# Bias rows added by TensorE, a shorter normalisation and a re-staged quantised FFN in a joined decoder kernel

## The reference

```python
def _layernorm(x, axis=-1, eps=1e-05):
    m = jnp.mean(x, axis=axis, keepdims=True)
    v = jnp.var(x, axis=axis, keepdims=True)
    return (x - m) / jnp.sqrt(v + eps)
...
    h = xmid + h                     # 128 features wide
    h = h @ w_up.T + b_up            # back to 1024
    return x_init + jnp.transpose(h, (1, 0, 2))
...
def _dynamic_quant(x, inv_smooth):
    xs = x.astype(jnp.float32) * inv_smooth
    scale = jnp.maximum(jnp.max(jnp.abs(xs), axis=-1, keepdims=True) / QMAX, 1e-08)
    q = jnp.clip(jnp.round(xs / scale), -QMAX, QMAX)
    return (q, scale)
...
    qg, sg = _dynamic_quant(x_flat, inv_gate)      # x_flat is bf16
    qu, su = _dynamic_quant(x_flat, inv_up)
    gate_out = _quant_gemm(qg, sg, w_gate, s_wgate)
    up_out = _quant_gemm(qu, su, w_up, s_wup)
    inter = jax.nn.silu(gate_out) * up_out
    inter = jnp.clip(inter, -SWIGLU_LIMIT, SWIGLU_LIMIT).astype(jnp.bfloat16)
    qi, si = _dynamic_quant(inter, inv_inter)
    out = _quant_gemm(qi, si, w_down, s_wdown)
```

## Time and profile before

| | before |
|---|---|
| median of 3 runs | 3969.88 us (3968.72 to 3972.8) |
| profiled execution, its own time | 3982.61 us |
| its span | 3980.8 us |
| PE busy | 3182.8 us (80%), mean granted clock 0.9 |
| DVE busy | 2233.0 us (56%) |
| ACT busy | 1579.2 us (40%) |
| POOL busy | 502.0 us (13%) |

### The profile page before, as it was taken

The page is one execution under the profiler, slowest core; times in us unless marked ns, Lnnn a source line. Parts: engine busy times, 40 slices in busy tenths (PEclk is TensorE's granted clock), DMA queues, the critical chain, the costliest instruction groups (busy, mean ns, idle before and its releaser), DMA issues. The chain is left out here.

```text
span 3980.8 us, 109362 instructions
## 1 busy us (share of the span) xinstructions
PE 3182.8 (80%) x43218; PEld 2136.2 (54%) x43218; DVE 2233.0 (56%) x5375; ACT 1579.2 (40%) x3982; POOL 502.0 (13%) x1854
## 2 busy tenths in 40 slices
PE   7556568644479999999688899999999999985797
PEld 4424135322256666666344666666666666662343
DVE  2656767578855555555421555555555555547455
ACT  2221134444522222222111566666666666652333
POOL 0000321133310000000000000000000000005232
PEclk9576679866789999999899999999999999996799
DMA  2000020110010000000101233333333333320100
GB/s 97 3 1 1 11 45 8 39 52 0 0 45 1 0 0 0 0 0 0 35 29 37 78 91 87 91 90 88 91 87 92 86 92 88 90 84 0 66 32 37
DMA packets 278942, 176.69 MB, mean 44 GB/s; under 512 B 14496, under 2 KB 268016, under 8 KB 278816
## 3 DMA queue, kind: packets, MB, share of 16 engines
q1 hardware_dynamic: 276128, 172.70, 14.8%
q0 software_dynamic: 2752, 3.18, 0.5%
HBM read 165.12 MB, written 13.90 MB: 45 GB/s over the span
## 5 line engine op out<-in xcount | busy, mean ns | idle before, releaser
L1828 PE MATMUL ps<-de_hg,st_at 128*32 128x128 f32 x16384 | 516.3, 275 | 0.3 <-DVE st_at L1990 0.3
L1828 PEld LDWEIGHTS ps<-de_hg,st_at 128*32 128x32 f32 x16384 | 424.5, 110 | 31.6 <-DVE st_at L1990 0.5
L1893 ACT ACTIVATE st_th<-ps,st_sw 128x128 f32<-128x128 f32 x1024 | 292.7, 368 | 248.0 <-PE ps L1800 248.0
L1973 DVE TENSOR_TENSOR st_th<-ps,st_sw 128x512 f32<-128x512 f32 x256 | 177.1, 692 | 155.5 <-PE ps L1800 155.5
L1766 POOL COPY de_ah<-st_at 128x8 f32 (+1 forms) x256 | 50.7, 198 | 1510.2 <-DVE st_at L1990 1510.2
L1247 PEld LDWEIGHTS ps<-sa_xt,w_wq 128*128 128x128 f32 x2048 | 234.7, 194 | 11.0 <-issue 9.2
L1247 PE MATMUL ps<-sa_xt,w_wq 128*128 128x128 f32 x2048 | 237.9, 278 | 1.9 <-ACT sa_xt L1363 1.9
L1318 PE MATMUL ps<-sa_wo,sa_ct 128*128 128x512 f32 x512 | 225.0, 598 | 13.1 <-issue 13.1
L1789 PE MATMUL ps<-st_hk,st_cwt 112*32 112x128 f32 x4096 | 164.7, 278 | 87.9 <-DMA st_hk<-padded_alignments 85.9
L2252 PE MATMUL ps<-rf_wb,rf_sp 128*128 128x512 bf16 x768 | 184.4, 394 | 20.1 <-DVEq L2383 20.1
L1800 PE MATMUL ps<-st_fs,st_waf 32*128 32x128 f32 x4096 | 186.5, 296 | 12.5
(11 more groups left out here) (415 smaller groups left out, 6341.3 us busy)
## 6 DMA issues: line engine op xcount, KB each, us to landing
st_hk<-padded_alignments SPq DMA_DIRECT2D x254, 448.0 KB, 3.6
X<-in_x_dram SPq DMA_DIRECT2D x16, 512.0 KB, 9.0
out_dram<-X SPq DMA_DIRECT2D x16, 512.0 KB, 2.7
w_wq<-in_Wq_perm_dram SPq DMA_DIRECT2D x1, 4096.0 KB
sa_wo<-in_Wo_perm_dram SPq DMA_DIRECT2D x1, 4096.0 KB, 14.2
gate_inputs<-dp_ro SPq DMA_DIRECT2D x16, 256.0 KB, 2.3
st_rin<-gate_inputs SPq DMA_DIRECT2D x128, 32.0 KB, 3.3
rf_wf<-in_weightT_dram SPq DMA_DIRECT2D x8, 512.0 KB, 8.0
```

The source lines that it names most:

```text
L1828: ins = pe.matmul(R[g][32 * q:32 * q + 32, :], at[g][:, b, :], hg[:, BG * g + b, q * P:(q + 1) * P], start=False, stop=(b == BG - 1), tile ...
L1893: ins = act.activation(th[g][:, b, :], sums(g, 0)[:, b // 2, (b % 2) * P:(b % 2 + 1) * P], ACT.Tanh, bias=sw[g][:, b:b + 1])
L1973: dve.tensor_tensor(th[g][:, 4:8, :].rearrange("p (k s) n -> p k s n", s=2), sums(g, 1).rearrange("p k (s n) -> p k s n", s=2), sw[g][:, 4 ...
```

## The change

It has three parts.

The normalisation. DVE makes only the statistics; the semaphore that released POOL after the fifth small operation now follows L99's successor directly. POOL makes four operations a tile in place of thirteen: minus the mean, variance plus epsilon, that to the power −0.5 (the operation `pow`), and the product of the two. All six normalising stages use it.

The bias rows. In `dn` and in `dp` POOL, which has nothing else to do there, makes three bf16 rows out of each fp32 bias row, whose sum is the bias: SP loads it into partitions 0, 32 and 64 of a cleared tile, and POOL casts, copies one row and subtracts, twice, over 128x1024. In `up` and `yy` each half tile gets a second matmul, of bf16 ones (128x128) with these rows (128x512), into the same PSUM bank. The addition of the bias on DVE and its broadcast load go.

The quantised FFN. The smoothing goes from POOL to DVE, next to the search for the scale, and `v` has one buffer for each of gate and up. TensorE turns the fp32 value that still carries the rounding constant; ACT takes the constant off as it copies the turned tile out of PSUM to bf16. The clips, the casts of L1000 and L1035 and DVE's copy L1066 go. The gate's sixteen turns become 8 + 4 before the gate and 4 between gate and up. DVE forms the row of tile b in the loop of tile b. SP loads the smoothing rows first.

```diff
-        link(dve.bn_aggr(self.agg[:, k, :], self.stats[:, k, :, :]))
-        v, y, nm = self.vy[:, k, 0:1], self.vy[:, k, 1:2], self.vy[:, k, 3:4]
-        link(dve.tensor_scalar(v, self.agg[:, k, 1:2], LN_EPS, None, ALU.add))
...
-        dve.tensor_scalar(nm, self.agg[:, k, 0:1], -1.0, None, ALU.mult).then_inc(self.var_done, 1)
+        dve.bn_aggr(self.agg[:, k, :], self.stats[:, k, :, :]).then_inc(self.agg_done, 1)
...
-        for step in range(3):
-            link(pool.tensor_tensor(q, y, y, ALU.mult))
-            link(pool.tensor_tensor(q, q, v, ALU.mult))
-            link(pool.tensor_tensor(q, q, self.c15[:, :], ALU.add))
-            link(pool.tensor_tensor(self.rs[:, k, 0:1] if step == 2 else y, y, q, ALU.mult))
+        pool.tensor_tensor(nm, self.agg[:, k, 0:1], minus, ALU.mult)
+        link(pool.tensor_tensor(v, self.agg[:, k, 1:2], eps, ALU.add))
+        link(pool.tensor_tensor(self.rs[:, k, 0:1], v, power, ALU.pow))
         pool.tensor_tensor(self.rs[:, k, 1:2], nm, self.rs[:, k, 0:1], ALU.mult).then_inc(self.rstd_done, 1)
...
+class BiasRows:
...
+        sp.wait_ge(self.cleared, 1)
+        for p in (0, 32, 64):
+            sp.dma_start(self.raw[p:p + 1, :], src.rearrange("(o n) -> o n", o=1)).then_inc(self.loaded, 16)
...
+        for p in (0, 32):
+            link(pool.tensor_copy(self.part[:, :], self.raw[:, :]))
+            link(pool.tensor_copy(self.rows[p:p + 1, :], self.part[p:p + 1, :]))
+            link(pool.tensor_tensor(self.raw[:, :], self.raw[:, :], self.part[:, :], ALU.subtract))
+        pool.tensor_copy(self.rows[64:65, :], self.raw[64:65, :]).then_inc(self.ready, 1)
...
+    def add(self, pe, out, h):
+        return pe.matmul(out, self.ones[:, :], self.rows[:, h * 512:(h + 1) * 512], start=False, stop=True)
...
-                            ins = pe.matmul(ps[:, 2 * (b % 2) + h, :], hm[:, b, :], w_up[:, h * 512:(h + 1) * 512],
-                                            start=True, stop=True)
+                            pe.matmul(ps[:, 2 * (b % 2) + h, :], hm[:, b, :], w_up[:, h * 512:(h + 1) * 512],
+                                      start=True, stop=False)
+                            ins = up_bias.add(pe, ps[:, 2 * (b % 2) + h, :], h)
...
-                            link(dve.tensor_tensor(r, r, b_up[:, :].unsqueeze(1), ALU.add))
...
+                for k in range(4):
+                    ins = pe.transpose(ps[:, (0, 1, 2, 0)[n], k * P:(k + 1) * P],
+                                       v[:, j, (4 * h + k) * P:(4 * h + k + 1) * P], ident[:, :])
+                ins.then_inc(t_done, 1)
...
+            def off(act, dst, src):
+                return act.activation(dst, src, ACT.Identity, bias=rnd[:, 1:2])
...
                     act.wait_ge(rci_done, b + 1)
                     act.activation(vi[:, :], vi[:, :], ACT.Identity, bias=rnd[:, 0:1], scale=rc[:, 2 + k:3 + k]).then_inc(added_i, 1)
...
+                    off(act, qit[:, :, :].rearrange("p k n -> p (k n)"), ps[:, TI, :]).then_inc(qit_done, 1)
+                    if has(b + 1):
+                        add_round(act, b + 1, 0)
+                        add_round(act, b + 1, 1)
+                        keep_gate(act, b + 1)
+                        keep_up(act, b + 1)
...
+                link(dve.tensor_tensor(v[:, j, :], xh[:, k, :], inv[:, j, :], ALU.mult))
+                if j == 1:
+                    dve.sem_inc(read, 1)
+                find_scale(dve, link, v[:, j, :], j, rc_done)
...
-                            link(dve.tensor_tensor(r, ps[:, 4 + 2 * k:6 + 2 * k, :].rearrange("p a n -> p (a n)"), lyb[:, :], ALU.add))
+                            link(dve.tensor_tensor(r.unsqueeze(1), ps[:, 4 + 2 * k:6 + 2 * k, :].rearrange("p a n -> p (a n)").unsqueeze(1),
+                                                   X[:, bass.ds(b, 1), :], ALU.add))
                             dve.sem_inc(o_used, 1)
-                            link(dve.tensor_tensor(r.unsqueeze(1), r.unsqueeze(1), X[:, bass.ds(b, 1), :], ALU.add))
```

More of the change, by code:

```diff
@@ L122, in apply, with __init__, work_in, load @@
                        bias=self.rs[:, k, 1:2], scale=self.rs[:, k, 0:1]).then_inc(self.row_free, 1)
+class BiasRows:
+    def __init__(self, kept):
+        self.rows = kept.sb("b3", [P, HID], BF16)
+        self.ones = kept.sb("ones16", [P, P], BF16)
+    def work_in(self, work):
+        self.raw, self.part = work.sb("b_raw", [P, HID]), work.sb("b_part", [P, HID], BF16)
+        self.cleared, self.loaded, self.seq, self.ready = work.sems("b_cleared b_loaded b_seq b_ready")
+    def load(self, sp, src):
+        sp.wait_ge(self.cleared, 1)
+        for p in (0, 32, 64):
+            sp.dma_start(self.raw[p:p + 1, :], src.rearrange("(o n) -> o n", o=1)).then_inc(self.loaded, 16)
+    def split(self, pool):
+        link = Chain(pool, self.seq)
+        pool.memset(self.raw[:, :], 0.0).then_inc(self.cleared, 1)
+        pool.memset(self.ones[:, :], 1.0).then_inc(self.ready, 1)
+        link(pool.memset(self.rows[:, :], 0.0))
+        pool.wait_ge(self.loaded, 48)
+        for p in (0, 32):
[3 more added lines that the diff above has]
+        pool.tensor_copy(self.rows[64:65, :], self.raw[64:65, :]).then_inc(self.ready, 1)
+        pool.wait_ge(self.ready, 2)
+    def add(self, pe, out, h):
+        return pe.matmul(out, self.ones[:, :], self.rows[:, h * 512:(h + 1) * 512], start=False, stop=True)
 SEQ = NB
@@ L928, in _ @@
             def _(pool):
-                pool.wait_ge(w_load, 96)
-                def smooth(b, k):
-                    pool.wait_ge(staged, b + 1)
-                    if not (isinstance(b, int) and b < 2):
-                        pool.wait_ge(q_done, 2 * b - 2)
-                    for j in range(2):
-                        pool.tensor_tensor(v[:, k, j, :], xh[:, k, :], inv[:, j, :], ALU.mult).then_inc(scaled, 1)
                 ln.start_pool(pool, Chain(pool, pool_seq))
-                for b in range(4):
-                    smooth(b, b % 2)
@@ L941, in _ @@
-                with pool.Fori(0, NB // 2 - 2) as i:
-                    link = Chain(pool, pool_seq, 1 + i * 2 * ln.POOL_LINKS)
+                with pool.Fori(0, NB // 2) as i:
+                    link = Chain(pool, pool_seq, ln.POOL_SETUP + i * 2 * ln.POOL_LINKS)
                     for k in range(2):
                         ln.factors(pool, link, 2 * i + k, k)
-                        smooth(2 * i + 4 + k, k)
-                link = Chain(pool, pool_seq, 1 + (NB - 4) * ln.POOL_LINKS)
-                for b in range(NB - 4, NB):
-                    ln.factors(pool, link, b, b % 2)
@@ L965, in _, with project @@
+            def project(pe, b, j):
+                pe.wait_ge(t_kept, 3 * b + (1, 3)[j])
+                if j == 0:
+                    pe.wait_ge(gu_used, b)
+                for k in range(KH):
+                    ins = pe.matmul(ps[:, GU + j, :], qt[:, j, k, :], (wu if j else wg)[:, k, :],
+                                    start=(k == 0), stop=(k == KH - 1))
+                ins.then_inc(gu_done, 1)
             @block.tensor
@@ new lines, in _, with body @@
+                dve.wait_ge(w_load, 64)
+                FIRST = 6
+                PER = 4 + 2 + 6 + 2 + ln.LINKS
+                state = {"link": link}
+                def body(b, k):
+                    link = state["link"]
+                    dve.wait_ge(gu_done, 2 * b + 1)
+                    dve.scalar_tensor_tensor(out=gu[:, 0, :], in0=ps[:, GU, :], scalar=sc[:, 0:1], in1=swg[:, :],
+                                             op0=ALU.mult, op1=ALU.mult).then_inc(gate_done, 1)
+                    dve.wait_ge(gu_done, 2 * b + 2)
+                    link(dve.scalar_tensor_tensor(out=gu[:, 1, :], in0=ps[:, GU + 1, :], scalar=sc[:, 1:2], in1=swu[:, :],
+                                                  op0=ALU.mult, op1=ALU.mult))
+                    dve.sem_inc(gu_used, 1)
+                    dve.wait_ge(silu_done, b + 1)
+                    link(dve.tensor_tensor(gu[:, 1, :], gu[:, 0, :], gu[:, 1, :], ALU.mult))
+                    link(dve.tensor_scalar(it[:, :], gu[:, 1, :], LIMIT, -LIMIT, ALU.min, ALU.max))
+                    dve.wait_ge(ti_done, b)
+                    link(dve.tensor_tensor(vi[:, :], it[:, :], invi[:, :], ALU.mult))
+                    find_scale(dve, link, vi[:, :], 2 + k, rci_done)
+                    if has(b + 1):
+                        for j in range(2):
+                            smooth(dve, link, b + 1, 1 - k, j)
```

249 lines of the change are left out of this document (103 added, 146 removed).

## The result

The changed kernel takes 3787.78 us (median of 4 runs, 3786.36 to 3788.87) beside 3969.3 us for the kernel before (4 runs): ratio 0.9542, 95% interval 0.9526 to 0.9559, 181.5 us less. The forecast was 3798 us, 171.5 less in its sum, with a range of 3778 to 3840.

The account below looks back on a forecast made before the run. DVE was taken to bound the upward projection and quantised FFN, TensorE the cross attention. Terms of 20.1, 42.1, 39.2, 14.3, 8.7, 0.3 and 46.8 sum to 171.5 us less, a median of 3798 us, range 3778 to 3840.

Parts of the forecast that it names:

- Tails, 20.1: After the last tile's statistics in six stages: 0.95 us of DVE and 2.4 of POOL go from each, 20.1 us.
- my two ends: Bounds for one `pow` on POOL: 0.19 us, which the prediction took, and 3.2 us from above.
- Upward projection 42.1: `up`: DVE sets the period, which falls from 5.61 to 3.07 us; with head and last tile 42.1 us less.
- epilogue 39.2: `yy`: the period falls from 5.69 to 3.17 us; with 1.5 us for the last tile 39.2 us less.
- Cross attention, 14.3: `ca`: five small operations ahead of DVE's copy of the turned probabilities go, 0.95 us in each of 15: 14.3 us.
- Routed FFN, 8.7: `rf`: ACT's cast no longer stands behind the norm's application, 0.62 us in each of 14 tiles: 8.7 us less.
- Self attention, 0.3: `sa`, which TensorE nearly fills: 0.3 us less beside its tail.
- Quantised FFN, 46.8: `ff`: head 9.9, loop 36.3 as the period falls from 20.0 to 17.6, rest of the tail 0.6: 46.8 us less.
- The chain that I summed: One tile of `ff`, DVE's scale, products and maxima through gate and up: 16.7 us, 17.6 with nine handoffs.
- Rival (b): In `ff` gate, or gate and up, run at 1.2 GHz: 24 to 52 us lost, 3822 to 3850; 12%.
- Building the rows, 0: POOL's seven operations in each of `dn` and `dp` are hidden: 0 us, up to 16 us each if not.
- Rival (d): The loops are held elsewhere, ACT or a barrier is next, and half of the gain stays: 3885; 6%.

Follow-up runs that it names:

- bias_only: The kernel before with only the bias rows on TensorE, its normalisation and FFN as before: 3926.98 us, ratio 0.9895.
- ffn_only: The kernel before with only the new quantised FFN: 3917.89 us, ratio 0.9876.
- norm_only: The kernel before with only the shorter normalisation: 3880.61 us, ratio 0.9781.
- unroll: The changed kernel with DVE's loops of `up` and `yy` written out instead of looped: 3772.08 us, ratio 0.9514.
- pipe: The kernel of unroll with its FFN reordered: TensorE makes the next tile's gate before this tile's down product, DVE smooths further ahead: 3730.84 us, ratio 0.9405.
- pool_smooth: The changed kernel with the smoothing of the quantised FFN back on POOL: 3786.91 us, ratio 0.9551.

## Why the prediction was right, and where its terms were off

*Tails, 20.1.* Right in kind. `pow` is 0.55 us, not 0.19. From the last aggregate to ACT it is 4.7 us before and 1.6 after in each of the six stages, so a tail gives 3.1 and the six 18.7. The lower of my two ends was the nearer, but wrong by a factor of three: the size of an operation, one element per partition, did not give its price.

*Upward projection 42.1 and epilogue 39.2.* Measured 42.8 and 42.4 with their tails, 39.7 and 39.3 without. The chain of 3.07 us was right but for the back edge, 0.36 us every second tile, which no row of before could show, since ACT's release was awaited there. The loops gave 15 × (5.61 − 3.25) = 35.4 us for my 38.1, and 36.0 for 37.8; in the epilogue its two ends made up for it, which is luck. That ACT's release is the next bound, as the prediction wrote, bias_only shows; it cost the one part alone 0.4 us a tile. TensorE kept the high level, as argued from the stage that is 79% busy: in the loop of `up` it stood at the low one for 61 us of 85 before and for under 1 us of 49 after.

*Cross attention, 14.3.* Measured 20.7 without the tail, the largest miss in a stage. The loop gave 18.0 us and the stage's start 2.7. The start need not be the change's: ffn_only, whose `up` and `ca` are those of before, gained 3.1 us there as well. That leaves 3.7 us in the loop. TensorE was at 1.2 GHz for 14 us of this loop before and for 3.5 after; it fell four times, and once. Three of the four falls came 0.6 us after a pause of 1.91 us, which is 1.05 after; the fourth came in a pause of 3.47 us, which is there in both and has the one fall of after 0.9 us behind it. At the low clock TensorE's work takes about twice its time (eight turns 1.9 us for 1.04), so 10.5 us less of it are about 10.5/2 = 5 us. My term counted the 0.95 us and not what a shorter pause does to the clock. norm_only shows the same gain and the same 3 us at the low level, bias_only shows neither (14 us), so it belongs to the shorter normalisation. unroll and pipe give a second price. Their `ca` is the code of the changed kernel, but its last stretch, from the pause of 3.47 us to the last row, has 6.8 us at the low clock for 3.4 and takes 13.7 and 13.6 us for 12.6: 1.0 to 1.1 us for 3.4, about 3.3 for 10.5. The 3.7 us lie between the two prices; that the falls account for all of them remains an estimate.

*Routed FFN, 8.7.* Measured 12.3 without the tail. ACT's cast no longer stands behind the norm, as forecast, and TensorE is at the low clock for 4 us of the loop where it was for 18. How the 12.3 divide between the two is open: bias_only, with the old normalisation, had 6 us less at the low clock and was only 1.1 us shorter.

*Self attention, 0.3.* Measured 2.0 with its tail of 3.1, so the rest got 1.1 us longer. Its period is 50.03 us for 49.94; norm_only has 49.93. Why is open.

*Quantised FFN, 46.8.* Measured 48.8 without the tail: the head gave 10.8 for 9.9, the loop 37.0 for 36.3. The period of 17.49 us fits the forecast 17.6 partly by luck. The chain that I summed takes 17.1 to 17.4 us where it is the bound; in six of fifteen steps it was not, and the steps of 17.6 to 18.3 brought the mean back up. Rival (b), gate and up at 1.2 GHz, did not come. The low clock fell on the down product and, in those steps, on the turns behind it. So the statement that the down product is hidden failed in six steps, for 5.1 us in all, and held by a hair in the others; pool_smooth, which took 2.5 us off my chain, found the other one in its place.

*Building the rows, 0.* POOL had the first rows ready at 41 us, within `dn`'s 65, and the second 27 us into `dp`. `dn` and `mx` end at 413.5 us after and 415.9 before (416.9 in the second profile of the changed kernel), `dp` is 0.6 us longer. Covered.

*Rival (d)*, that other engines hold the loops, holds for bias_only, where ten tiles waited for ACT, and not for the whole change.

## What to carry to other kernels

A sum along one chain tells what goes when that chain is shortened only as far as the next one, so write that one down too, with its length. In the FFN here two chains lay within a microsecond of each other: taking 2.5 us off the one (pool_smooth) gave 0.06 us a tile, and changing the order, so that the gate's turns no longer stand behind the down product, gave 2.8. Where two edits meet in one loop, as the normalisation and the bias rows did, measure each alone: they added up but for 0.16 us a tile. And once a loop's stalls are gone, its back edge and its waits on register values are the next thing: written out, tiles of 3.25 us became 2.91.

## What was not expected of the hardware

- `pow` on POOL over 128x1 takes 0.55 us in all six stages (0.547 to 0.559 in 96), and the next operation follows 0.63 us after its start; a product takes 0.19.
- The written-out stream: 0.12 us from an aggregate's start to that of the next row, 0.29 in the loop, and 0.36 us at the back edge.
- While POOL multiplies 128x1024, DVE's addition of two SBUF rows took 2.53 us in the median (up to 3.15) for 1.23, and a clip of 512 columns with bf16 output 2.10 in the mean for 0.43. The Trainium skill ("SBUF — State Buffer", "Who interferes with whom") calls the pair of ports that the two share an exclusive lock, held for the whole instruction; the held durations agree with it, since none is longer than the unheld one plus one product of POOL, 2.14 us.
- fp32 turns were seen at the high clock again: eight in 1.07 us in pipe, where eight took 1.9 in a low stretch of the changed kernel. The Trainium skill ("TensorE: Matmul & The Clock Gate", "Part 4: PE-mode transpose") has the full clock not engage for them; here they run at it, though no run shows them raising it alone.
